# Row sums of a block's exponentials on TensorE, the last exponentials ahead of all SiLUs, and fp32 sums in passes of 256 columns

## What is computed

```python
xn = layernorm(x)
s  = attention(xn)          # 16 heads of size 8, a latent K/V; softmax over the 16 heads of a token
g  = silu(ffn(xn))          # block attention + mixture of experts
out = x + s * g

# attention: q, k, v of (8, 512, 16, 8)
att = softmax(einsum('bthd,btgd->bthg', rope(q), rope(k)) / sqrt(8))
out = einsum('bthg,btgd->bthd', att, v) @ Wout + bout

# ffn, on S = 8 positions ("sequence") and 512 "batch" entries
qkv = layernorm(xn) @ qkv_weight.T          # 4 groups of 4 query heads
attn = softmax(causal(q k^T / sqrt(8)));  h1 = xn + (attn v) @ proj_weight.T
probs = softmax(layernorm(h1) @ router);  top 2 of 8 experts, capacity 1280
moe = gelu(xt @ w1[e]) @ w2[e];           ffn = h1 + scattered moe
```

## Time and profile before

| | us |
|---|---|
| median of 3 runs | 496.65 (493.86 to 496.85) |
| the profiled execution, its own time | 496.27 |
| its span, first to last instruction | 494.5 |
| VectorE busy | 381.8 (77%) |
| TensorE matmul busy | 346.7 (70%) |
| GpSimd busy | 254.8 (52%) |
| ScalarE busy | 172.5 (35%) |

### The profile page before, as it was taken

One profiled execution on the slowest core, in us unless ns is written; L12 is line 12 of the kernel. 1 busy time (PEld: TensorE's weight loads), 2 busy tenths in 40 slices (PEclk: granted clock), 3 DMA queues, 4 the chain that ended last, 5 costly groups with the idle time before them and its releaser, 6 DMA issues.

```text
span 494.5 us, 4714 instructions
## 1 busy us (share of the span) xinstructions
PE 346.7 (70%) x1518; PEld 250.5 (51%) x1518; DVE 381.8 (77%) x505; ACT 172.5 (35%) x382; POOL 254.8 (52%) x282
## 2 busy tenths in 40 slices
PE   1478886577466843316749998887798696769994
PEld 1455665356355310015628686575566564524752
DVE  5998999779799900005999998899999599790494
ACT  3473834515260100000101422754664654511310
POOL 0578736000067777786000385776786676545602
PEclk9878997869656775555958999897988987977996
DMA  8999500000011111129000210241233211129301
GB/s 200 178 216 288 163 1 1 0 2 0 0 38 55 54 50 52 54 64 258 2 0 0 56 47 28 55 125 59 77 103 88 80 58 37 39 77 342 87 0 42
DMA packets 53558, 38.06 MB, mean 77 GB/s; under 512 B 5337, under 2 KB 50206, under 8 KB 53534
## 3 DMA queue, kind: packets, MB, share of 16 engines
q1 hardware_dynamic: 48926, 28.25, 22.6%
q0 software_dynamic: 4608, 9.51, 5.7%
HBM read 16.55 MB, written 21.20 MB: 76 GB/s over the span
## 4 chain that ended last, share of the span: by engine, by line
PE 28%; DVE 25%; issue 13%; another core or an unknown queue 12%; ACT 5%; DMA 1%; SPq 0%; DVEq 0%; ACTq 0%
PE banks L944 6%; PE banks L916 6%; DVE prod L276 5%; DVE score L615 4%; DVE prod L285 4%; PE banks L923 3%; PE banks L969 3%; PE banks L777 2%; DVE prod L273 2%; PE banks L802 1%; PE banks L957 1%; PE banks L909 1%; ACT flat L1240 1%; PE banks L955 1%
## 5 line engine op out<-in xcount | busy, mean ns | idle before, releaser
L1314 POOL DMA_INDIRECT slot_rows<-rows_all,scatter_at x64 | 61.8, 966 | 75.3 <-DVE scatter_at L590 56.1
L1357 POOL DMA_INDIRECT expert_rows<-flat,to_at x80 | 79.8, 998 | 31.3 <-issue 20.9
L285 DVE TENSOR_TENSOR prod<-score,banks 128x2048 f32<-128x2048 f32 x16 | 35.6, 2282 | 55.6 <-remote 55.5
L944 PE MATMUL banks<-prod,c_identf 128*128 128x256 f32 x256 | 63.3, 405 | 19.2 <-issue 18.8
L944 PEld LDWEIGHTS banks<-prod,c_identf 128*128 128x128 f32 x256 | 52.1, 205 | 31.8 <-issue 23.5
L1301 POOL TENSOR_TENSOR prod<-rows_all,block_kv 128x64 f32<-128x64 f32 (+3 forms) x64 | 48.7, 800 | 32.6 <-ACT block_kv L1086 32.5
L276 POOL TENSOR_TENSOR qkv_h<-block_kv,qkv_h 128x2048 f32<-128x2048 f32 x8 | 35.9, 4506 | 52.4 <-DVE score L603 49.3
L916 PE MATMUL banks<-flat 128*128 128x512 f32 (+1 forms) x96 | 42.5, 592 | 7.7 <-ACT flat L1226 5.4
L276 DVE TENSOR_TENSOR prod<-banks,qkv_h 128x2048 f32<-128x2048 f32 x20 | 44.8, 2284 | 0.6 <-DVE score L615 0.2
L615 DVE TENSOR_REDUCE score<-prod 128x512 f32<-128x4096 f32 x10 | 44.2, 4420 | 0.3
L802 PE MATMUL banks<-wx,qkv_h 128*128 128x128 f32 x192 | 35.1, 353 | 10.1 <-ACT qkv_h L1105 4.2
(11 more groups left out here) (190 smaller groups left out, 581.3 us busy)
## 6 DMA issues: line engine op xcount, KB each, us to landing
slot_rows<-prod SPq DMA_DIRECT2D x10, 528.0 KB, 10.8
flat<-slot_rows SPq DMA_DIRECT2D x16, 264.0 KB
expert_rows<-prod SPq DMA_DIRECT2D x8, 512.0 KB, 6.3
flat<-expert_rows SPq DMA_DIRECT2D x8, 512.0 KB, 7.5
xn_all<-in_x SPq DMA_DIRECT2D x4, 512.0 KB, 4.8
flat<-in_w SPq DMA_DIRECT2D x16, 128.0 KB
out<-rows_all SPq DMA_DIRECT2D x7, 256.0 KB, 2.3
expert_rows<-flat,to_at POOLq DMA_INDIRECT x80
```

The source lines that it names most:

```text
L285: return eng.tensor_tensor(value_pair(s, a // 2)[:, a % 2, :].rearrange("p (h g d) -> p h g d", g=H, h=H), p.unsqueeze(3).broadcast_to([P, ...
L944: i = M.matmul(head_bank(s)[:, 2 * p * D:2 * (p + 1) * D].rearrange("p (a h d) -> p a h d", a=2, h=H), C["identf"][:], value_pair(s, p).re ...
L1314: Q.indirect_dma_start(slots_d, bass.IndirectOffsetOnAxis(ap=scatter_at[:, k, n:n + 1], axis=0), z2x[:, h, s, part], None, element_offset= ...
L1357: Q.indirect_dma_start(expert_d, bass.IndirectOffsetOnAxis(ap=to_at[:, e % 2, a:a + 1], axis=0), ye[:, e % 2, a, :], None).then_inc(ye_out ...
```

## The change

- **Front.** The row sum of the exponentials (L457 on VectorE, semaphore `s_sum`) is gone. TensorE sums the eight columns of `sc2[par]` against the identity, 8 matmuls of 64 columns, into the last quarter of bank 7 (`exp_sums(u)`, `exp_total(par)`), and VectorE takes the reciprocal from there, after a wait for `exp_summed`. New waits for it stand ahead of the difference into `sc2`, ahead of `residual`, and, of `s_rsum`, in `project_block`.
- **Middle.** `sum_scores` makes passes of 256 columns instead of 512, so twice as many matmuls.
- **Tail.** `exponentials(7)` stands ahead of all SiLUs on ScalarE; before, it stood behind six. Five banks (0, 1, 2, 3, 7) are used instead of four, five batches are summed ahead of `sum_values(6, .)` instead of six, and each sum is made in passes of 256 columns. The two banks of the last transposes and of the last outputs change.

```diff
-TAIL_BANKS = 4
-LAST_TURNED, LAST_OUT = (6, 0), (1, 2)
+TAIL_BANK, FIRST_TAILS = (0, 1, 2, 3, 7, 0, 1, 2), 5
+LAST_TURNED, LAST_OUT = (6, 3), (0, 1)
...
+        def exp_total(par):
+            at = 3 * T // 4 + par * 2 * S * QH
+            return bank[PROJ_GROUPS[-1][0]][:, at:at + 2 * S * QH].rearrange("p (l m) -> p l m", l=2)
...
# VectorE, scores_of_unit
                 dve.wait_ge(W["s_max"], u + 1)
+                wait_past(dve, "exp_summed", u - 1)
                 V.tensor_tensor(sc2[par], sc, smax.unsqueeze(3).broadcast_to([P, 2, S * QH, S]), ALU.subtract).then_inc(W["s_diff"], 1)
# VectorE, values_of_unit
                 dve.wait_ge(W["s_exp"], u + 1)
-                wait_past(dve, "unit_kept", u - 1)
-                V.tensor_reduce(ssum[par], sc2[par], AX_X, ALU.add).then_inc(W["s_sum"], 1)
...
-                dve.wait_ge(W["s_sum"], u + 1)
-                V.reciprocal(ssum[par], ssum[par]).then_inc(W["s_rsum"], 1)
+                dve.wait_ge(W["exp_summed"], u + 1)
+                wait_past(dve, "unit_kept", u - 1)
+                V.reciprocal(ssum[par], exp_total(par)).then_inc(W["s_rsum"], 1)
# VectorE, residual
+                dve.wait_ge(W["exp_summed"], min(2 * h + 4, 2 * TT))
# TensorE
+            def exp_sums(u):
+                par = u % 2
+                pe.wait_ge(W["wpx_kept"], 1)
+                wait_past(pe, "proj_read", u // 2 - 1)
+                wait_past(pe, "s_rsum", u)
+                pe.wait_ge(W["s_exp"], u + 1)
+                for t in range(S):
+                    i = M.matmul(exp_total(par), C["identf"][:], sc2[par][:, :, :, t], start=(t == 0), stop=(t == S - 1))
+                i.then_inc(W["exp_summed"], 1)
# project_block
                 wait_past(pe, "proj_read", h)
+                pe.wait_ge(W["s_rsum"], min(2 * h + 3, 2 * TT))
# the order on TensorE
+            exp_sums(0)
             value_sums(0)
             project_rows(2, (1, 0))
+            exp_sums(1)
             value_sums(1)
             turn_normed(0)
             turn_twice_normed(3)
+            exp_sums(2)
             turn_block(0)
             value_sums(2)
             project_block(0)
             project_rows(3, (3, 2))
+            exp_sums(3)
             value_sums(3)
             project_rows(3, (1, 0))
             turn_normed(1)
+            exp_sums(4)
             turn_block(1)
             value_sums(4)
             project_block(1)
             turn_normed(2)
+            exp_sums(5)
             value_sums(5)
             turn_normed(3)
+            exp_sums(6)
             turn_block(2)
             value_sums(6)
             project_block(2)
+            exp_sums(7)
             value_sums(7)
...
# sum_scores
-                for d in range(HD):
-                    i = M.matmul(bank[SCORE_BANK[p]].rearrange("p (a m) -> p a m", a=2), C["identf"][:],
-                                 score_pair(PE_SCORES, p).rearrange("p a (d m) -> p d a m", d=HD)[:, d], start=(d == 0), stop=(d == HD - 1))
+                for a in range(2):
+                    for d in range(HD):
+                        i = M.matmul(bank[SCORE_BANK[p]][:, a * H * H:(a + 1) * H * H], C["identf"][:],
+                                     score_pair(PE_SCORES, p)[:, a, d * H * H:(d + 1) * H * H], start=(d == 0), stop=(d == HD - 1))
...
# the tail on TensorE
-                wait_past(pe, "silu_done", s - TAIL_BANKS + 1)
+                wait_past(pe, "silu_done", s - FIRST_TAILS + 1)
...
                 for k in range(TOPK):
-                    i = M.matmul(bank[s % TAIL_BANKS].rearrange("p (a d) -> p a d", a=TT), C["identf"][:], yg[:, s, :, k, :], start=False, stop=(k == TOPK - 1))
+                    for a in range(0, TT, 2):
+                        i = M.matmul(bank[TAIL_BANK[s]][:, a * D:(a + 2) * D].rearrange("p (a d) -> p a d", a=2), C["identf"][:], yg[:, s, a:a + 2, k, :], start=False, stop=(k == TOPK - 1 and a == TT - 2))
...
-            q_bank = TAIL_BANKS - 1
-            q_read(max(i for i in range(S) if Q_BANK[i] == q_bank))
-            for s in range(TAIL_BANKS):
+            q_read(6)
+            pe.wait_ge(W["attn_done"], 6)
+            for s in range(FIRST_TAILS):
                 tail_start(s)
-            for s in range(TAIL_BANKS):
-                tail_sum(s)
-            for s in range(TAIL_BANKS, 6):
-                tail_start(s)
+            for s in range(FIRST_TAILS):
                 tail_sum(s)
             sum_values(6, 0)
             sum_values(6, 1)
-            for s in range(6, S):
+            for s in range(FIRST_TAILS, S):
                 tail_start(s)
                 tail_sum(s)
# the tail on ScalarE
             keep_attention(5)
-            for s in range(6):
-                gates(s)
             exponentials(7)
-            for s in range(6, S):
+            for s in range(S):
                 gates(s)
```

More of the change, by code:

```diff
@@ L213, in build @@
             moments spread_done dev_done off_done zb_done zb_part xn_done turned turn_kept piece_ready piece_kept ratio_done
-            qk_prod qk_score s_max s_diff s_exp s_sum s_rsum v_placed pv_prod pv_ready unit_kept
+            qk_prod qk_score s_max s_diff s_exp exp_summed s_rsum v_placed pv_prod pv_ready unit_kept
             proj_ready h1_done proj_read spread2_done dev2_done off2_done z2_done row_of_logits
@@ L960, in tail_start @@
             def tail_start(s):
-                wait_past(pe, "silu_done", s - TAIL_BANKS + 1)
-                M.matmul(bank[s % TAIL_BANKS].rearrange("p (a d) -> p a d", a=TT), C["identf"][:], xn_all[:, :, s, :], start=True, stop=False)
+                wait_past(pe, "silu_done", s - FIRST_TAILS + 1)
+                M.matmul(bank[TAIL_BANK[s]].rearrange("p (a d) -> p a d", a=TT), C["identf"][:], xn_all[:, :, s, :], start=True, stop=False)
             def tail_sum(s):
@@ L1257, in gates @@
                 act.wait_ge(W["v_ready"], s + 1)
-                A.activation(v_all[:, s, :], bank[s % TAIL_BANKS], ACT.Silu).then_inc(W["silu_done"], 1)
+                A.activation(v_all[:, s, :], bank[TAIL_BANK[s]], ACT.Silu).then_inc(W["silu_done"], 1)
             keep_k(1)
```

## The result

The changed kernel takes **511.84 us** (median of 4 runs, 510.08 to 513.49) where the kernel before takes 495.32 (4 runs, 493.86 to 496.85): a ratio of **1.033**, 95% interval 1.028 to 1.039. It is slower. The profiled execution took 511.74 us with a span of 509.9, so 15.4 more than the span before.

A forecast was written before the change was run, and what follows sets the result against it. No engine was taken to bound the whole; VectorE bounds the front, TensorE close behind. 496.3 + 14.4 (front) + 3.7 (middle) - 0.9 (tail) = 513.5, given as 513 us; own range 505 to 521, widened to 499 to 524.

The forecast's parts named there:

- the likeliest case: Whole kernel: slower, 513 us, from a longer front and middle and a slightly shorter tail; chance 0.68.
- (a): Rival, front: TensorE is in time for each `exp_sums`, so the kernel gets faster, 490.6 us; chance 0.06.
- (c): Rival, middle: TensorE's stall goes away or breaks off as the fetch falls elsewhere, about 470 to 480 us; chance 0.08.
- The walk of the front: Front: both engines followed unit by unit, VectorE's reciprocals waiting for late TensorE blocks; front 14.4 us longer.
- the first block: Front, `exp_sums(0)`: starts at 41.8 us, takes 3.3 us, and VectorE waits 8.7 us for it.
- the new waits' place decides: Front: what decides is where the new waits stand, since VectorE runs in order behind each reciprocal.
- The step that counted instructions: Middle: the stall counts instructions, so 26 `sum_scores` records are left and VectorE waits 3.7 us for the second sum.
- The signs given for the stall's ends: Middle: the stall starts near TensorE's instruction fetch at 152 to 155 us, ends with GpSimd's unbroken work at 227.84.
- The 0.9: Tail: one start of 0.86 us leaves TensorE's chain, so the end moves by -0.9 us.
- only the first block is late: Rival, front: later blocks are in time; +3 - 0.9, and 0 to 3.7 in the middle, 498 to 502; chance 0.10.
- The third: Rival, middle: VectorE's wait of 55 us goes or breaks off, about 470 to 480 us; chance 0.08.
- The fourth: Rival, front and middle: strided columns cost double or the stall takes more, 521 to 530 us; chance 0.08.

The follow-up runs named there:

- window_after: Changed kernel with batch 1's score sums and batch 0's value sums made by VectorE instead of TensorE; 481.23 us, 0.970 of the kernel before.
- late_recip: Changed kernel with the reciprocal and its wait for the block moved to the start of `keep_unit` of the same unit; 511.12 us, 1.028 of the kernel before.
- earlier_sums: Changed kernel with the `exp_sums` blocks of units 1, 3 and 5 moved earlier in TensorE's order; 517.83 us.
- mid_only: Kernel before with only the middle part, `sum_scores` in passes of 256 columns; 503.0 us, ratio 1.013.
- late_units_dve: Changed kernel with the sums of units 0, 1, 2, 3, 5 and 7 back on VectorE; 498.05 us, 1.003 of the kernel before.
- dve_window: Kernel before with batch 1's score sums and batch 0's value sums made by VectorE instead of TensorE; 469.51 us, ratio 0.949.
- tail_only: Kernel before with only the tail part of the change; 500.06 us, ratio 0.999.

## Why the prediction held, step by step

**The sum.** Predicted 513, measured 511.84; slower, as the likeliest case said. By stages of the profiled executions: front +14.4 predicted, +16.8 in the trace (13.7 by front length); middle +3.7 against +1.5; experts 0 against -1.3; tail -0.9 against -1.5. The errors are small and partly cancel, and that is luck in part: 3.1 of the front's 16.8 us are the late copy, which the walk didn't have and the change didn't make, and they stand in for what the middle fell short. Without them the profiled execution would be near 508.6, still inside the range. (The upper end of that range is not what its terms give: 20 in the front and 8 in the middle make 523, not 521. And (a) and (c) make 0.14, not 0.13.)

**The walk of the front** was right in its places: the reciprocals named (0, 2, 3, 5, 7) wait and 4 and 6 don't. The keeps were walked to 55.3, 67.1, 79.8, 91.5, 102.6, 114.4 and 124.5, and ended at 58.96, 69.02, 81.45, 92.97, 103.94, 115.47 and 127.04. The term that was mis-sized is the first block: a wait of 12.04 us instead of 8.7, since it started at 44.88 instead of 41.8, behind constant products at half the clock. In `window_after`, whose copy stands at 41.63, that wait is 9.01, so the walk itself was close. Later blocks were put at 1.8 us and measured 2.06; the nearest row, of 8 columns, was a fair price. Not foreseen: unit 1 waits too, 1.46 us. The gap (3.7 at the first keep) had shrunk to 1.1 at the sixth and was 2.5 at the seventh.

**The reading of its cause** was narrower than the runs allow. The prediction says that the new waits' place decides. `late_recip` and `earlier_sums` move place and order; one gains 2.1 us, the other none by its end. The walk gave the right number because it counted TensorE's work too; the statement that holds is that TensorE, close behind VectorE in this stage, was given 18 us more work to save VectorE 5.

**The middle.** The step that counted instructions holds in kind: VectorE asks for its second sum and waits, 1.53 us in the changed kernel, 2.88 in `mid_only`, 2.59 and 2.75 in `late_recip` and `late_units_dve`. 20 records were left where 26 were predicted. The signs given for the stall's ends don't hold: the fetch is not its start, and GpSimd's run of work is not its end. By the Trainium skill, Runtime: NRT & Kernel Launch, Instruction fetch mechanics, a fetch is mostly hidden; the prediction set the trace against it, and was wrong to do so as to the fetch, which lies behind the first late result of the changed kernel. The wait of 1.53 us came from the number of matmuls in the stall, which the page doesn't speak of.

**The tail.** Both halves held: the wait of 18.8 us was no path, and `pv_summed` took its place. The 0.9 is the start that was left out, and it measures 0.86. TensorE's chain is 1.5 us shorter in the whole changed kernel and 3.4 with the tail part alone (33.85 to 30.4); what goes beyond 0.9 is the clock of the first sums, whose 40 records took 10.84 us in the one and 8.90 in the other. The prediction had put no clock into that term.

**The rivals.** That TensorE is in time (faster, 490.6) and that only the first block is late (498 to 502) are refuted by the waits. The third, the stall breaking off, did not happen by the change. Its price was about right: with the longer front it was put at 470 to 480, and `window_after`, in which VectorE no longer waits for TensorE there, takes 481.23. The fourth (521 to 530) needed a block of 3.5 us or a longer wait in the middle; neither came.

## What to carry to other kernels

Before work is moved off the busiest engine, add it to the list of the engine that receives it, stage by stage: an instruction of 0.68 us became a block of 2.06 us on an engine that was 80% busy in that stretch, and a handshake between them (1.35 us and more) came on top. A wait that vanishes when it is moved is a matter of placement. If it turns up elsewhere, take the work itself away and double it: what comes back, and what is added, says what the work costs. And look first at the largest wait whose length follows somebody else's work: here 55 us, and giving VectorE work of its own there was worth 5% (469.5 us against 496.9), where the tail part alone gave a ratio of 0.999.

## What the runs showed of the hardware

**TensorE and the scatters.** While GpSimd issues indirect scatters (64 in 81 us), results of TensorE reach the others late. The first late copy on ScalarE stands 17 to 24 us behind the first scatter in all fourteen traces; TensorE then comes down to one matmul record each 2.8 us, whether of 512 or 256 columns; and all is released 5 to 10 us behind the last scatter. VectorE and GpSimd run on (VectorE 99% busy in `dve_window`, each scatter 0.96 us throughout). What holds TensorE is open: the runs exclude its instruction fetch as the start and GpSimd's next product as the end, and no more.

**TensorE's clock in the front.** The same instructions run at one of two clocks, 2.4 GHz (1.00) or 1.2 GHz (0.50), by when the clock is lowered. In `tail_only`, whose front is that of the kernel before, it is low through the constant products:

```profile
41.00:45.00 4.00, 3.27 (x10) 1.91 (x10) 3.93 (x11) 1.11 (x4) 4.00 (x7) 0.50 1.21 208
45.00:50.00 5.00, 5.00 (x17) 3.81 (x18) 4.25 (x11) 2.80 (x11) 5.00 (x8) 0.50 1.10 320
```

Its copy that sets `wpx_kept` is at 49.08 us against 41.59 in the earlier trace rows, and the first keep ends at 56.8 instead of 48.0 (51.8 in `mid_only`). Two things add up in that. One is the clock: in five traces the copy stands at 44.7 to 45.7, with VectorE on time until then and TensorE's matmuls ahead of the copy at 0.50. The other is VectorE, in the three traces with the copy at 49.1. There TensorE made the first pieces of `qkv` sooner (16 records in 3.24 us, in the eleven others 4.66 to 5.58), GpSimd began its products earlier and ran on without a gap, and VectorE's normalization beside them took twice as long, which puts everything behind it 3.4 us later. First before, then `tail_only`:

```profile
16.47 3.04 DVE L413 TENSOR_SCALAR xn_all<-xn_all,mom 128x128 f32<-128x128 f32 x8
```

```profile
16.76 6.12 DVE L413 TENSOR_SCALAR xn_all<-xn_all,mom 128x128 f32<-128x128 f32 x8
```

That the two engines hinder each other there is argued from these traces and was not tried. Between 33 and 37 us TensorE was busy 2.73 of 4 us in `tail_only` at a mean clock of 0.81, and in the kernel before 1.93 of 4 at 1.00; what decides when the clock falls was not tried either. So in the seven traces with the front of the kernel before the index is done anywhere from 134.3 to 146.5 us, and a difference of two profiled spans is worth reading only stage by stage, from a common instruction.

**Matmuls of few columns.** A record of 64 columns with a stride of 8 elements takes 0.13 us at the full clock (2.06 us for 16) and 0.23 at half (3.68), where one of 256 columns takes 0.22 (13.98 us for 64, L971). A fourth of the columns saves only 40% of the time, so sums of small rows are dear on TensorE.
